# A Mamba block and a mixture-of-experts layer on one core: three of sixteen scan states weighted by C in channel layout and added to y by transfers instead of being transposed

## The chip, the core and the metric

One core of a Trainium2 chip runs the whole program. The metric is the device time of one execution in microseconds; lower is better. The kernel before took 2412.94 us (median of three runs, 2410.59 to 2414.03).

## What is computed

The reference takes a batch of 16 sequences of 512 tokens with 256 channels and applies two layers, each as `x + layernorm(layer(layernorm(x)))`. The first is a selective state-space (Mamba) layer, the second a gated low-rank mixture with a cumulative sum over time. The change lies in the first:

```
h = x * rsqrt(mean(x*x) + eps) * norm_scale @ w_in
xs, res = split(h);  res = silu(res);  xs = silu(causal_conv(xs) + conv_b)
delta, B, C = split(xs @ w_xproj);     delta = softplus(delta @ w_dt + b_dt)
deltaA = exp(delta * -exp(A_log));     deltaBx = delta * xs * B
ys = scan over time of (ys = deltaA * ys + deltaBx)      # 512 channels x 16 states
y  = sum over the 16 states of ys * C
out = (y + xs * D) * res @ w_out
```

All is float32.

## The kernel before

Layout. The 512 inner channels lie on the 128 partitions in four chunks c, time (512 steps) along the free dimension. The program keeps three stages in flight, each for another sequence: F (the front: norm, w_in, convolution, silu, delta, B, C), the scan over the 16 states, and B and L (the output projection, both layernorms, router, and the expert layer). Every engine runs one fixed, in-order program.

Order. `BEATS` is 128: a period of one sequence has 16 slots, one for each state n, and a slot has 8 beats. `TIMETABLE` (L96) gives each task of F, B and L on each engine a beat, modulo 128; `walk` (L391) runs for every beat first the engine's `scan_part` and then the tasks of that beat, for the sequence that is then in that stage. A beat is a place in the order and no time: engines meet only through semaphores.

The scan, for state n in slot n:

- ScalarE (L1260) computes `decay = exp(delta * rate)` for chunk c at beats 0, 2, 4, 6 into two PSUM tiles used in turn. It may be two chunks ahead of VectorE.
- GpSimd (L775) computes `bx = dx * B` for two chunks at a time at beats 0 and 4 into a ring of three (`BX_RING`), so it may be up to three half slots ahead. It needs the row of B for state n, spread over all partitions.
- SyncE (L611) loads that row from a scratch in DRAM into a ring of four (`BB_RING`), three slots ahead; `write_B` (L590) puts B there when F has computed it.
- VectorE (L1405) runs the scan of chunk c at beats 0, 2, 4, 6 into `h[n % 2]`, and at beats 1, 3, 5, 7 the products of the state before: `yT += stateT * C` (L1441), for four chunks of tokens.
- TensorE (L991) supplies these: it transposes `h` of the state before, four 128x128 blocks for each of four token chunks, into two PSUM tiles `stateT` used in turn. C is then one number per partition (`C_tok`).
- When all 16 states are summed, `y_task` (L889) transposes yT back, `u_task` (L1340) adds `xs * D`, and `o_task` on GpSimd multiplies by `res`.

In stage L, `cum_task` (L1230, ScalarE) writes `cum_sb`, `pr_task` (L1399, VectorE) multiplies into `prod`, and `pt_task` on TensorE transposes `prod`. For the first sequence `prod` also holds a piece of the raw weights. `rows` of the next sequence's B are loaded by the task `row`, w, w2, d1 and dx (L691 to L718) are the GpSimd steps that finish delta and `dx = delta * xs` for the next sequence, four chunks each, and `silu_task` (L1125) and `gelu_task` (L1209) are long blocks of ScalarE with a table load at both ends.

## Time and profile before

The profiled execution took 2413.96 us, with a span of 2412.2 us from the first to the last instruction.

| engine | busy us | share of the span | instructions |
|---|---|---|---|
| VectorE (DVE) | 2147.9 | 89% | 2775 |
| TensorE (PE) | 2143.7 | 89% | 9268 |
| GpSimd (POOL) | 1898.4 | 79% | 1369 |
| ScalarE (ACT) | 1839.0 | 76% | 3893 |
| DMA engines (16) | 14% of their time, all issued by SyncE | | |

How to read it: the shares include a filling and an emptying of the pipeline at both ends, in which VectorE is nearly idle, so the steady periods in between are fuller than the shares say. A duration in the profile runs until the instruction's last write; the next one on the same engine starts a little before that, so what an instruction costs its engine is the distance from start to start. A wait is put down to the instruction that came last.

### The profile page before, as it was taken

The numbers are of one execution on the slowest core, as the hardware profiler recorded it, in microseconds if no ns is written. First come the engines' busy times: TensorE is split into PE (matmuls) and PEld (weight loads), VectorE is DVE, ScalarE is ACT, GpSimd is POOL, SyncE is SP. The second block draws the span as 40 slices with busy tenths as digits, with TensorE's granted clock in tenths as the row PEclk, the third lists the DMA queues.
The fourth block names the chain that finished last, engine by engine and source line by source line (L and its number), as shares of the span: only waits on it lengthen the run. The fifth ranks groups of instructions, "written<-read, shape, count | busy, mean of one in ns | idle before, by whom it ended". The sixth has DMA issues, their size and how long they took to land.

```text
span 2412.2 us, 35956 instructions
## 1 busy us (share of the span) xinstructions
PE 2143.7 (89%) x9268; PEld 1300.3 (54%) x9268; DVE 2147.9 (89%) x2775; ACT 1839.0 (76%) x3893; POOL 1898.4 (79%) x1369
## 2 busy tenths in 40 slices
PE   5687899999998989899998999999898999998888
PEld 2455455564655556465655646565564656555454
DVE  2889999998999999999999989999999999999920
ACT  6675787869698787968778696978879797875644
POOL 1679797988889798888979888897988889796520
PEclk8796899898999989999999989999899999989899
DMA  6111101111111011111102011110211110011000
GB/s 135 36 45 39 45 32 32 58 31 54 37 57 33 27 61 30 54 36 58 33 27 62 30 52 37 58 36 23 64 32 54 36 58 31 26 51 35 27 9 9
DMA packets 83401, 101.70 MB, mean 42 GB/s; under 512 B 23480, under 2 KB 49872, under 8 KB 83168
## 3 DMA queue, kind: packets, MB, share of 16 engines
q1 hardware_dynamic: 83168, 99.06, 13.7%
q8 instruction: 89, 1.46, 0.2%
q14 instruction: 144, 1.18, 0.2%
HBM read 90.13 MB, written 8.91 MB: 41 GB/s over the span
## 4 chain that ended last, share of the span: by engine, by line
DVE 34%; issue 26%; PE 15%; ACT 13%; POOL 9%; DVEq 1%; ACTq 0%; POOLq 0%
DVE h L1425 15%; DVE yT L1441 11%; PE bank L827 7%; POOL bx L792 4%; PE stateT L1007 4%; ACT decay L1277 2%; DVE xs L1336 2%; PE bank L986 1%; DVE yT L1438 1%; POOL dx L718 1%; POOL delta L712 1%; ACT scratch L1207 1%; ACT res L1141 1%; ACT prodT L1064 1%; ACT o_rows L1045 1%
## 5 line engine op out<-in xcount | busy, mean ns | idle before, releaser
L792 POOL TENSOR_TENSOR bx<-dx,B_rows 128x1024 f32<-128x1024 f32 x512 | 1204.6, 2363 | 286.9 <-DVE h L1425 252.4
L1425 DVE TENSOR_TENSOR_SCAN h<-decay,bx 128x512 f32<-128x512 f32 x1024 | 1236.8, 1208 | 64.7 <-ACT decay L1277 51.9
L1277 ACT ACTIVATE decay<-delta,decay_rate 128x512 f32<-128x512 f32 x1024 | 702.4, 691 | 351.0 <-DVE h L1425 343.0
L1007 PE MATMUL stateT<-ident,h 128*128 128x128 f32 x4096 | 646.9, 291 | 176.2 <-DVE h L1425 119.3
L1007 PEld LDWEIGHTS stateT<-ident,h 128*128 128x128 f32 x4096 | 492.6, 148 | 523.4 <-issue 306.8
L1441 DVE SCALAR_TENSOR_TENSOR yT<-stateT,C_tok,yT 128x512 f32<-128x512 f32 x960 | 694.7, 724 | 47.7 <-PE stateT L1007 47.5
L827 PE MATMUL bank<-hT,w_in_sb 128*128 128x512 f32 x512 | 246.5, 611 | 23.5 <-DVE xs L1336 9.9
L827 PE MATMUL bank<-q_to_expert,xnT 128*128 128x512 f32 x512 | 261.5, 638 | 0.1
L827 PE MATMUL bank<-k_to_expert,cumT 128*128 128x512 f32 x512 | 258.4, 630 | 0.0
L986 PE MATMUL bank<-expert_to_out,prodT 128*128 128x256 f32 x1024 | 244.5, 382 | 6.4 <-issue 6.4
L1241 ACT ACTIVATE cum_sb<-bank,gate 128x64 f32<-128x64 f32 x1024 | 221.8, 326 | 22.9 <-PE bank L827 20.2
L986 PEld LDWEIGHTS bank<-expert_to_out,prodT 128*128 128x128 f32 x1024 | 185.8, 191 | 31.0 <-issue 10.9
L827 PEld LDWEIGHTS bank<-hT,w_in_sb 128*128 128x128 f32 x512 | 91.7, 194 | 106.5 <-issue 73.0
L827 PEld LDWEIGHTS bank<-q_to_expert,xnT 128*128 128x128 f32 x512 | 97.3, 207 | 80.1 <-issue 79.5
L827 PEld LDWEIGHTS bank<-k_to_expert,cumT 128*128 128x128 f32 x512 | 92.8, 202 | 78.7 <-issue 72.8
L827 PE MATMUL bank<-w_out_sb,res 128*128 128x256 f32 x512 | 121.9, 382 | 0.0
L688 POOL TENSOR_TENSOR xs<-xs,scratch 128x511 f32<-128x511 f32 (+2 forms) x93 | 106.8, 1148 | 18.4 <-ACT scratch L1110 12.3
L1403 DVE TENSOR_TENSOR prod<-bank,cum_sb 128x512 f32<-128x512 f32 x128 | 85.2, 665 | 37.0 <-PE bank L827 24.9
L827 PE MATMUL bank<-xnT,q_to_router 128*128 128x512 f32 x256 | 117.9, 594 | 0.0
L827 PEld LDWEIGHTS bank<-w_out_sb,res 128*128 128x128 f32 x512 | 94.5, 192 | 17.6 <-issue 7.2
L1251 ACT ACTIVATE prodT<-bank 128x512 f32<-128x512 f32 x128 | 75.9, 593 | 30.1 <-PE bank L986 25.3
L736 POOL TENSOR_TENSOR res<-xs,res 128x512 f32<-128x512 f32 x64 | 80.9, 1276 | 20.4 <-DVE xs L1343 20.4
(164 smaller groups left out, 2584.8 us busy)
## 6 DMA issues: line engine op xcount, KB each, us to landing
B_rows<-B_scratch SPq DMA_DIRECT2D x256, 256.0 KB, 3.2
x_front<-in_L_attn_x SPq DMA_DIRECT2D x16, 512.0 KB, 5.3
x_back<-in_L_attn_x SPq DMA_DIRECT2D x16, 512.0 KB, 3.5
out<-x_back SPq DMA_DIRECT2D x16, 512.0 KB, 5.8
w_in_sb<-in_L_attn_w_in SPq DMA_DIRECT2D x1, 1024.0 KB, 5.9
cum_sb<-in_L_ffn_V_fwd SPq DMA_DIRECT2D x2, 256.0 KB
prod<-in_L_ffn_W_inv_exp SPq DMA_DIRECT2D x2, 256.0 KB
xnT<-in_L_ffn_W_fwd SPq DMA_DIRECT2D x2, 256.0 KB
```

Of the source, the lines that this page charges most:

```text
L688: pool.tensor_tensor(xs[b.parity][:, c, back:], xs[b.parity][:, c, back:], scratch[:, tile, 0:T - back], ALU.add).then_inc(f_pool.step(f"c ...
L736: pool.tensor_tensor(res[r][:, c, :], xs[r][:, c, :], res[r][:, c, :], ALU.mult).then_inc(b_pool.step(f"o{c}"), 1)
L792: pool.tensor_tensor(bx[use % BX_RING][:, :, :], dx[q.parity][:, 2 * half:2 * half + 2, :], row, ALU.mult).then_inc(s_bx.step(f"{n},{half} ...
L827: last = pe.matmul(out_ap, lhsT, rhs, start=(i == 0), stop=(i == len(pairs) - 1))
L986: last = pe.matmul(use.bank[:, 0:D], prodT[:, 4 * br + i, :], expert_to_out[:, 4 * br + i, :], start=(br == 0 and i == 0), stop=False)
L1007: last = pe.transpose(stateT[j % 2][:, c * P:(c + 1) * P], h[n % 2][:, c, j * P:(j + 1) * P], ident[:, :])
L1241: last = act.activation(cum_sb[u % 2][:, k * RK:(k + 1) * RK], use.bank[:, k * RK:(k + 1) * RK], ACT.Copy, scale=gate[:, j, br * KE + k:br ...
L1251: act.activation(flat(prodT[:, 4 * br:4 * br + 4, :]), use.bank[:, :], ACT.Copy).then_inc(l_act.step(f"pt{u}"), 1)
L1277: act.activation(decay[c % 2][:, :], delta[q.parity][:, c, :], ACT.Exp, scale=decay_rate[:, c, n:n + 1]).then_inc(s_exp.step(f"{n},{c}"), 1)
L1403: dve.tensor_tensor(prod[u % 2][:, :], use.bank[:, :], cum_sb[u % 2][:, :], ALU.mult).then_inc(l_dve.step(f"pr{u}"), 1)
L1425: dve.tensor_tensor_scan(h[n % 2][:, c, :], decay[c % 2][:, :], bx[(2 * n + c // 2) % BX_RING][:, c % 2, :], 0.0, ALU.mult, ALU.add).then_ ...
L1441: ins = dve.scalar_tensor_tensor(out=yT[:, k, :], in0=stateT[k % 2][:, :], scalar=C_tok[batch.parity][:, k, n:n + 1], in1=yT[:, k, :], op0 ...
```

## The change

States 3, 7 and 11 (`MIXED`) are no longer transposed. For such a state n:

- SyncE loads the row of C for it, spread over the partitions, into `C_rows` (`row_of_C`, beat 4 of slot n-2); the scratch in DRAM now takes B and C.
- ScalarE copies `C_rows` into the PSUM tile `stateT[0]` at beat 7 of slot n (`spread_C`), after the product of state n-1 for token chunk 2 has read it.
- VectorE multiplies two chunks of `h` at a time by it in slot n+1: chunks 2 and 3 in place at beat 1, chunks 0 and 1 into `weighted` at beat 5 (`weigh_half`). The four products with `yT` fall away.
- GpSimd issues two transfers, 512 KB each, that add these halves to `xs` (`add_half`, `accum_op=ALU.add`): at beat 7 of slot n+1 and at beat 3 of slot n+2. Before the second it waits until the first has landed. VectorE's scan of state n+2, chunk 2, waits for the first to land, since it reads the same buffer.
- TensorE leaves out the 16 transposes of slot n+1.

So that `xs` can take these sums, ScalarE first scales it by D (`skip`, four tasks, after `dx`), and `u_task` is a plain addition. For the memory, `prod` goes (the product is written over `cum_sb`), and the ring of B rows has three places instead of four, so that the rows of B for states 0 and 1 of the next sequence are loaded early and row 0 must wait for `bx` of state 15. Many beats of the timetable are moved by some places.

```diff
-BB_RING = 4
+BB_RING = 3
+MIXED = (3, 7, 11)
+PLAIN = [n for n in range(NS) if n not in MIXED]
+C_AT, ADDED_AT = 7, (7, 3)
...
-    ("F", "silu", "act"): (67,),
+    ("F", "silu", "act"): (66,),
...
-    ("F", "w", "pool"): (97, 106, 120, 121),
-    ("F", "w2", "pool"): (99, 111, 123, 127),
-    ("F", "d1", "pool"): (102, 112, 127, 128),
-    ("F", "row", "sp"): (123, 127, 137),
+    ("F", "w", "pool"): (97, 103, 108, 123),
+    ("F", "w2", "pool"): (100, 105, 117, 124),
+    ("F", "d1", "pool"): (101, 107, 126, 126),
+    ("F", "row", "sp"): (113, 113),
...
+    ("F", "skip", "act"): (117, 122, 132, 132),
...
-    ("L", "pr", "dve"): (355, 368, 371, 384, 398, 430, 432, 438),
+    ("L", "pr", "dve"): (362, 371, 373, 387, 399, 425, 431, 441),
...
-    ("F", "dx", "pool"): (117, 118, 128, 129),
+    ("F", "dx", "pool"): (102, 123, 128, 131),
...
+            def add_half(q, n, half):
+
+                before = 2 * MIXED.index(n) + 1 - half
+                pool.wait_ge(s_mul.sem, s_mul.done(q, f"{n},{half}"))
+                pool.sem_inc(passed["pool"], 1)
+                if before == 0:
+                    pool.wait_ge(f_act.sem, f_act.done(q, "sk3"))
+                    pool.sem_inc(passed["pool"], 1)
+                if before or q.shift(-1).exists:
+                    pool.wait_ge(y_added, q.count(32 * len(MIXED), 16 * before))
+                    pool.sem_inc(passed["pool"], 1)
+                half_rows = flat(xs[q.parity][:, 2 * half:2 * half + 2, :])
+                source = flat(h[n % 2][:, 2:4, :]) if half else flat(weighted[:, :, :])
+                pool.dma_start(half_rows, source, accum_op=ALU.add).then_inc(y_added, 16)
+
             def scan_part(q, n, beat):
+                if q.exists and beat == ADDED_AT[0] and n - 1 in MIXED:
+                    add_half(q, n - 1, 1)
+                if q.exists and beat == ADDED_AT[1] and n - 2 in MIXED:
+                    add_half(q, n - 2, 0)
...
+            def spread_C(q, n):
+                act.wait_ge(C_in, q.count(16 * len(MIXED), 16 * (MIXED.index(n) + 1)))
+                act.sem_inc(passed["act"], 1)
+                act.wait_ge(s_acc.sem, s_acc.done(q, f"{n - 1},2"))
+                act.activation(stateT[0][:, :], C_rows[:, :], ACT.Copy).then_inc(s_C.step(f"{n}"), 1)
+
...
+            def weigh_half(q, n, half):
+
+                dve.wait_ge(s_C.sem, s_C.done(q, f"{n}"))
+                state = h[n % 2][:, 2 * half:2 * half + 2, :]
+                dve.wait_ge(s_scan.sem, s_scan.done(q, f"{n},{2 * half + 1}"))
+                if half == 0 and (MIXED.index(n) or q.shift(-1).exists):
+                    dve.wait_ge(y_added, q.count(32 * len(MIXED), 32 * MIXED.index(n)))
+                spread = stateT[0][:, :].rearrange("p (o t) -> p o t", o=1).broadcast_to([P, 2, T])
+                dve.tensor_tensor(state if half else weighted[:, :, :], state, spread, ALU.mult).then_inc(s_mul.step(f"{n},{half}"), 1)
...
                     if c == 0:
                         free = q if n >= 2 else q.shift(-1)
-                        if free.exists:
+                        if free.exists and n - 2 not in MIXED:
                             dve.wait_ge(s_tr.sem, s_tr.done(free, f"{(n - 2) % NS},{TB - 1}"))
+                    if c == 0 and n - 2 in MIXED:
+                        dve.wait_ge(s_mul.sem, s_mul.done(q, f"{n - 2},0"))
+                    if c == 2 and n - 2 in MIXED:
+                        dve.wait_ge(y_added, q.count(32 * len(MIXED), 32 * MIXED.index(n - 2) + 16))
...
+                if n in MIXED:
+                    if k % 2 == 0:
+                        weigh_half(batch, n, 1 - k // 2)
+                    return
```

## Rows read from the trace of the kernel before

**Rows 1.** Instructions on tile x_back: min/median/max ns, first and last start
```profile
L609 SPq MOVE out<-x_back x12: 29/29/29, 430.6 to 1969.6; - x12
```
**Rows 2.** Window: us, busy PE, PEld, DVE, ACT, POOL (count), clock, DMA share, GB/s
```profile
1115.00:1252.00 137.00, 127.20 (x562) 77.81 (x563) 130.63 (x170) 109.89 (x236) 119.99 (x86) 0.95 0.13 42
```
**Rows 3.** Waits between 430 and 2074 us: us in total, times, longest
```profile
DVE h L1425 <- ACT decay L1277: 39.2, 35, 1.7
DVE yT L1441 <- PE stateT L1007: 27.3, 29, 1.5
POOL bx L792 <- DVE h L1425: 158.5, 119, 5.0
```
**Rows 4.** VectorE's timeline in slots 12 and 13: start us, duration us, instruction
```profile
1145.93 0.68 DVE L1403 TENSOR_TENSOR prod<-bank,cum_sb 128x512 f32<-128x512 f32 x1
1146.53 1.21 DVE L1425 TENSOR_TENSOR_SCAN h<-decay,bx 128x512 f32<-128x512 f32 x1
1147.66 0.72 DVE L1441 SCALAR_TENSOR_TENSOR yT<-stateT,C_tok,yT 128x512 f32<-128x512 f32 x1
1148.31 1.21 DVE L1425 TENSOR_TENSOR_SCAN h<-decay,bx 128x512 f32<-128x512 f32 x1
```
**Rows 5.** Groups of instructions, VectorE: count | busy us, mean ns | idle before, releaser
```profile
L1441 DVE SCALAR_TENSOR_TENSOR yT<-stateT,C_tok,yT 128x512 f32<-128x512 f32 x960 | 694.7, 724 | 47.7 <-PE stateT L1007 47.5
L1357 DVE SCALAR_TENSOR_TENSOR rows<-x_back,r_keep,bank 128x256 f32<-128x256 f32 x64 | 29.5, 463 | 9.3 <-PE bank L827 9.3
```
**Rows 6.** VectorE's timeline, three waits of one period: in brackets the idle time before
```profile
1112.54 1.22 DVE L1425 TENSOR_TENSOR_SCAN h<-decay,bx 128x512 f32<-128x512 f32 x1 [1.45 <-ACT decay L1277]
1141.72 0.75 DVE L1441 SCALAR_TENSOR_TENSOR yT<-stateT,C_tok,yT 128x512 f32<-128x512 f32 x1 [1.23 <-PE stateT L1007]
1155.96 0.75 DVE L1441 SCALAR_TENSOR_TENSOR yT<-stateT,C_tok,yT 128x512 f32<-128x512 f32 x1 [1.13 <-PE stateT L1007]
```
**Rows 7.** TensorE's timeline: four transposes of a state
```profile
1180.07 0.60 PE L1007 MATMUL stateT<-ident,h 128*128 128x128 f32 x4
```
**Rows 8.** Groups of instructions, ScalarE, same columns
```profile
L1183 ACT ACTIVATE scratch<-scratch,one 128x512 f32<-128x512 f32 x64 | 46.3, 723 | 4.0
L1198 ACT ACTIVATE xnT<-bank 128x512 f32<-128x512 f32 x32 | 19.0, 594 | 0.1
```
**Rows 9.** Groups of instructions, GpSimd, same columns
```profile
L792 POOL TENSOR_TENSOR bx<-dx,B_rows 128x1024 f32<-128x1024 f32 x512 | 1204.6, 2363 | 286.9 <-DVE h L1425 252.4
L697 POOL TENSOR_TENSOR scratch<-scratch 128x512 f32<-128x512 f32 x60 | 76.0, 1272 | 0.5
```
**Rows 10.** GpSimd's timeline, its only waits for VectorE between 1273 and 1312 us
```profile
1273.25 2.38 POOL L792 TENSOR_TENSOR bx<-dx,B_rows 128x1024 f32<-128x1024 f32 x1 [0.41 <-DVE h L1425]
1309.56 2.36 POOL L792 TENSOR_TENSOR bx<-dx,B_rows 128x1024 f32<-128x1024 f32 x1 [0.94 <-DVE h L1425]
```
**Rows 11.** The page's DMA issues: count, KB each, us from issue to landing
```profile
B_rows<-B_scratch SPq DMA_DIRECT2D x256, 256.0 KB, 3.2
x_front<-in_L_attn_x SPq DMA_DIRECT2D x16, 512.0 KB, 5.3
x_back<-in_L_attn_x SPq DMA_DIRECT2D x16, 512.0 KB, 3.5
out<-x_back SPq DMA_DIRECT2D x16, 512.0 KB, 5.8
```
**Rows 12.** Instructions on tile x_back, columns as in group 1: the longest issue
```profile
L530 SPq DMA_DIRECT2D x_back<-in_L_ffn_U_inv x2: 1123/1134/1145, 28.1 to 29.3; - x2
```
**Rows 13.** SyncE's timeline: start us, duration us of a short issue
```profile
1129.57 0.39 SPq L589 DMA_DIRECT2D x_front<-in_L_attn_x  x1
```
**Rows 14.** Windows of 4 us in slots 11 and 13, columns as in group 2
```profile
1132.00:1136.00 4.00, 3.97 (x12) 2.68 (x12) 3.66 (x7) 3.97 (x8) 3.73 (x3) 0.50 0.91 302
1148.00:1152.00 4.00, 2.35 (x11) 2.06 (x12) 4.00 (x6) 3.83 (x7) 3.44 (x3) 0.52 0.22 70
1152.00:1156.00 4.00, 4.00 (x14) 2.16 (x13) 2.87 (x4) 3.87 (x8) 4.00 (x3) 0.63 0.00 0
```

More of the change, by code:

```diff
@@ L132 @@
-    ("B", "r", "dve"): (285, 289, 290, 291),
-    ("B", "st", "dve"): (293,),
+    ("F", "hT", "pe"): (21, 22),
+    ("F", "hT", "act"): (28, 29),
+    ("F", "x", "sp"): (90,),
+    ("F", "xs", "pe"): (29, 33, 36, 38),
+    ("F", "xs", "act"): (33, 35, 39, 42),
+    ("F", "cvA", "dve"): (32, None, 36, None),
+    ("F", "cvB", "dve"): (33, None, 37, None),
+    ("F", "cvC", "dve"): (34, None, 39, None),
+    ("F", "tap", "act"): (None, 37, None, 42),
+    ("F", "cv", "pool"): (None, 39, None, 62),
@@ new lines @@
+    ("F", "res", "pe"): (37, 41, 44, 55),
+    ("F", "res", "act"): (40, 50, 51, 59),
+    ("F", "silu", "act"): (66,),
+    ("F", "proj", "pe"): (77,),
+    ("F", "proj", "act"): (81,),
+    ("F", "B", "sp"): (85,),
+    ("F", "Ct", "pe"): (116,),
+    ("F", "Ct", "act"): (116,),
+    ("F", "dt", "pe"): (83, 85, 88, 104),
+    ("F", "dt", "act"): (87, 93, 104, 109),
+    ("F", "ex", "act"): (89, 97, 106, 110),
+    ("F", "ln", "act"): (91, 100, 106, 111),
+    ("F", "w", "pool"): (97, 103, 108, 123),
@@ L147 @@
+    ("B", "xnT", "act"): (318, 318),
+    ("B", "cum", "dve"): (319, 320),
+    ("B", "rt", "pe"): (320, 325, 325, 325),
+    ("B", "rt", "act"): (324, 325, 331, 331),
     ("B", "gelu", "act"): (334,),
@@ L289, in program @@
         cum_sb = [sb(f"cum_sb{i}", P, KR) for i in range(2)]
-        prod = [sb(f"prod{i}", P, KR) for i in range(2)]
+        weighted = sb("weighted", P, 2, T)
+        C_rows = sb("C_rows", P, T)
         prodT = sb("prodT", P, 8, P)
@@ L326, in program @@
         s_scan = Steps(sem("s_scan"), [f"{n},{c}" for n in range(NS) for c in range(CT)])
-        s_tr = Steps(sem("s_tr"), [f"{n},{c}" for n in range(NS) for c in range(TB)])
-        s_acc = Steps(sem("s_acc"), [f"{n},{c}" for n in range(NS) for c in range(TB)])
+        s_tr = Steps(sem("s_tr"), [f"{n},{c}" for n in PLAIN for c in range(TB)])
+        s_acc = Steps(sem("s_acc"), [f"{n},{c}" for n in PLAIN for c in range(TB)])
+        s_C = Steps(sem("s_C"), [f"{n}" for n in MIXED])
+        s_mul = Steps(sem("s_mul"), [f"{n},{half}" for n in MIXED for half in (1, 0)])
+        C_in, y_added = sem("C_in"), sem("y_added")
         b_pe = Steps(sem("b_pe"), steps_of("pe", "B", {"y": ["y{}"], "wo": ["wo{}"], "xnT": ["xnT{}"], "rt": ["rt{}"],
@@ L442, in walk @@
                 period(Batch(q))
-        stage_V = [cum_sb, prod]
+        stage_V = [cum_sb, [dx[1][:, t, :] for t in range(DT)]]
         stage_W = [[xnT[:, 0, :], xnT[:, 1, :]], [prodT[:, 4 * t:4 * t + 4, :].rearrange("p a b -> p (a b)") for t in range(DT)]]
@@ L609, in store, with row_of_C @@
                 sp.dma_start(batch.dram(out_rows), x_back[batch.parity][:, :, :]).then_inc(stored[batch.parity], 16)
+            def row_of_C(q, i):
+                free, last = (q, i - 1) if i else (q.shift(-1), len(MIXED) - 1)
+                if i == 0:
+                    sp.wait_ge(B_out, q.count(16, 16))
+                    sp.sem_inc(passed["sp"], 1)
+                if free.exists:
+                    sp.wait_ge(s_C.sem, s_C.done(free, f"{MIXED[last]}"))
+                    sp.sem_inc(passed["sp"], 1)
+                n = NS + MIXED[i]
+                sp.dma_start(C_rows[:, :], B_dram[q.parity, n:n + 1, :].partition_broadcast(P).rearrange("p o t -> p (o t)")).then_inc(C_in, 16)
             def scan_part(q, slot, beat):
+                if beat == 4 and q.exists and slot + 2 in MIXED:
+                    row_of_C(q, MIXED.index(slot + 2))
                 if beat == 0 and q.exists:
@@ L998, in scan_part @@
                     return
+                if n in MIXED:
+                    return
                 if j == 0:
                     pe.wait_ge(s_scan.sem, s_scan.done(batch, f"{n},{CT - 1}"))
-                back = n * TB + j - 2
+                at = PLAIN.index(n)
+                back = at * TB + j - 2
                 free = batch if back >= 0 else batch.shift(-1)
+                if j == 0 and n - 1 in MIXED:
+                    pe.wait_ge(s_mul.sem, s_mul.done(batch, f"{n - 1},0"))
+                    pe.sem_inc(passed["pe"], 1)
                 if free.exists:
-                    pe.wait_ge(s_acc.sem, s_acc.done(free, f"{back % (NS * TB) // TB},{back % TB}"))
+                    back %= len(PLAIN) * TB
+                    pe.wait_ge(s_acc.sem, s_acc.done(free, f"{PLAIN[back // TB]},{back % TB}"))
                 for c in range(CT):
@@ L1262, in scan_part @@
                     rates()
+                if q.exists and beat == C_AT and n in MIXED:
+                    spread_C(q, n)
                 if not q.exists or beat % 2:
```

123 lines of the change are left out of this document (54 added, 69 removed), and 6 rows, old and new, of the table TIMETABLE.

## Prediction

> **What bounds the kernel now.** I read the engines' shares first, then the period, then the waits. The stores of twelve inner sequences start 430.6 to 1969.6 us, so one sequence costs (1969.6 - 430.6) / 11 = 139.9 us [rows 1]. The scans of all 16 sequences run at about that rate, and a saving per period counts about 16 times; the filling and the emptying at the ends have little to do with the change. In a steady window VectorE is busy 130.6 of 137 us, TensorE 127.2, GpSimd 120.0, ScalarE 109.9 [rows 2]. Scaled to the period VectorE has 6.5 us of idle time, GpSimd 17, ScalarE 28. So VectorE is the bound, and its idle time says who holds it. From 430 to 2074 us (11.75 periods) it waited 39.2 us for ScalarE's decay, which is 3.3 a period, and 27.3 for TensorE's transposes, 2.3 a period [rows 3]. Of the first kind is the wait of 1.45 us at the silu block, of the second are those in slots 12 and 13 (1.23 and 1.13) [rows 6]. GpSimd waits 158.5 / 11.75 = 13.5 us a period for VectorE to free the ring [rows 3]: it is ahead, but the trace shows no such wait from 1273 to 1309.5, where the steps for the next sequence lie (slots 11 to 15) [rows 10]. There it has nearly nothing to spare.
>
> **VectorE's work.** From start to start a scan takes 1147.66 - 1146.53 = 1.13 us, a product with yT 0.65, and an addition or multiplication of 512 columns with one PSUM operand 0.60 [rows 4]. A multiplication over 1024 columns isn't in the trace. 256 columns more cost 724 - 463 = 261 ns in the mean durations [rows 5], so 512 more cost 0.52 and the new instruction 1.12, at least; the most is two of the old ones, 1.20. I take 1.13. Removed are 3 x 4 = 12 products, 7.80 us; added 3 x 2 = 6 weighings, 6.78; the four additions of u get cheaper by 0.05 each, 0.20. That is **-1.2 us a period** (bounds -0.8 to -1.3). The product of stage L costs the same; its buffer's wait moves to ScalarE.
>
> **TensorE.** 48 transposes of a period go, in 12 groups of four that take some 0.60 us each [rows 7], up to 7 us. VectorE's wait of 1.23 at slot 12 is for the transposes of state 11, which are left out; that of 1.13 in slot 13 comes after TensorE has fallen behind, and the missing slot-12 transposes give it 2.4 us. Of 2.3 us a period I expect all but 0.2 to go: **-2.1** (bounds -2.3 and 0, if TensorE's other tasks, moved by the timetable, take its place). What is late next is ScalarE.
>
> **ScalarE.** Three copies of C at 0.59 and four scalings of xs at 0.72 [rows 8] are 4.7 us of 28 idle. The copy in beat 7 of slot n can only start when VectorE is through beat 5; behind it on ScalarE is the decay for slot n+1, chunk 0, which VectorE needs after one scan and one product (1.78 us), against the copy's 0.59 and one decay of much the same size: a margin of some half a microsecond, which another ScalarE task in between uses up. Scaling chunk 1 (beat 122) waits for GpSimd's dx at beat 123, which is safe only while GpSimd is ahead. The silu block holds decay chunk 2 of slot 8 as before, since scan, weighing and cumulative scans take about the place of scan, product and cumulative scans. I take **+0.5** (bounds 0 and +2, the latter three lost margins and a late scaling).
>
> **SyncE.** Three C rows of 256 KB more, and row 0 of B must now wait for bx of state 15 and takes 3.2 us to land [rows 11]. GpSimd has three steps of 1.27 us [rows 9] between these two bx, 3.8 us, which hide it; without that cover it would cost up to 3.5 us a period. Nothing that is needed sooner stands behind the waiting load. Zero.
>
> **GpSimd and the transfers.** Six transfers a period that add are issued by GpSimd; the trace has none of that kind. Issue: between 0.39 and 1.13 us, the short and the long issue of SyncE [rows 12, 13]; I take 0.8, so 4.8 us of 17 idle. Landing, D: plain transfers of 512 KB take 3.5, 5.3 and 5.8 us [rows 11]; an adding one also reads its target, so the bounds are 3.5 and twice the longest, 11.6. I take 5.3, the one into SBUF that is slower, because SBUF on both sides saves a trip to DRAM and the second read costs some of that. Behind these waits on GpSimd's queue stand bx and the steps of the next sequence, and VectorE waits for bx. The Trainium skill, DMA: Bandwidth & Descriptors, section Anatomy of one DMA, gives 2.0 us plus the bytes at 436 GB/s for a transfer issued by GpSimd, an estimate of 3.2 us here; no transfer of this trace is issued so, and the sum by it would be -26 us or better in place of the -16 below.
>
> Let T be the end of VectorE's first weighing, in slot n+1. VectorE then has four scans (12,1), (12,2), (12,3), (13,0), a weighing, a product, scan (13,1) and a product before scan (13,2), which needs the second bx of state 13: 5 x 1.13 + 1.13 + 2 x 0.65 = 8.1 us, plus one task of stage L (0.60), so T + 8.7. GpSimd after T: issue 0.8, w 1.27, bx 2.36, w2 1.27, so T + 5.7; the landing is at T + 0.8 + D = 6.1; issue, d1 and bx, 0.8 + 1.27 + 2.36, end at T + 10.5. A **stall of 1.8 us** after state 11. After state 7 GpSimd has no steps of the next sequence: 6.1 + 0.8 + 2.4 = T + 9.3 against 8.1 + the silu wait of about 1.5 = 9.6, none. After state 3 three convolution sums of GpSimd and six taps of VectorE are both in the way: about T + 10 against 12, none. So **+1.8**; the other two bounds: D = 3.5 gives 1.4 (GpSimd's steps, not D, are then the limit), D = 11.6 gives 8.1 + 5.9 + 3.6 = 17.6.
>
> **Sum.** -1.2 - 2.1 + 0.5 + 1.8 = -1.0 us a period, times 16 = -16 us; the stall at slot 13 also gives ScalarE and TensorE time to catch up for the boundary, which I put at 0.2 a period, so -19. The profiled execution took 2413.96 us with a span of 2412.2, within 0.05% of the median 2412.94, so the sum can be put on the median: **2394 us** (-0.8%).
>
> **The rivals.** (a) *Landing is slow (slower).* The place is GpSimd's wait for the first half before it issues the second, with bx behind it. The stall after state 11 is D - 3.5, after state 7 D - 5.7, after state 3 D - 8. The other terms give -3.0 a period, so the sum turns at D = 6.1, where the first two make 3.0. At D = 8 they are 4.5 + 2.3 = 6.8, that is +3.8 a period, 2474 us; at 11.6 it is 2413 + 16 x 14.6 = 2647. For it: 6.1 is only 0.3 above a plain store. Against: SBUF is at both ends, and the DMA engines are 14% busy.
> (b) *TensorE's clock.* The granted clock is 0.50 from 1132 to 1136 and 0.52 from 1148 to 1152, that is 1.2 in place of 2.4 GHz; in the second case TensorE was busy only 2.35 of 4 us, and in the next window, at 0.63 with 4.00 busy, VectorE was left with 2.87 of 4 [rows 14] and waited 1.13 [rows 6]. The change takes 16 transposes out of slots 4, 8 and 12 and leaves holes there. With one more such stretch in each the 2.1 us stay and 3 x 1.2 come on top: -1.0 + 2.1 + 3.6 = +4.7 a period, 2488 us; with one more stretch, 2.3 a period, 2450. Against: stages F and L fill slot 4 and 12. The Trainium skill, TensorE: Matmul & The Clock Gate, Part 1, says that the throttled clock is the default and activity releases it; by that rule a relief of TensorE can be given back, and the row of 1148 agrees, that of 1132 (3.97 busy) doesn't by itself.
> (c) *Both hidden.* GpSimd does the steps while it would have waited for T, and the stall after state 11 is gone: -3.0 a period, 2365 us.
> (d) *Nothing moves.* ScalarE's bound (+2) and the stall eat the gain: -1.2 - 2.1 + 2 + 1.8 = +0.5, with the margins half kept, 0: 2413 us.
>
> **How the numbers follow.** Forecast 0.36, (c) 0.19, (a) 0.24, (b) 0.08, (d) 0.13. A difference of 0.2% (5 us) is about what a measurement of this kernel can tell from none. Faster is the forecast and (c), 0.55; within 0.2% is (d), 0.13; slower is (a) and (b), 0.32. The range goes from 2358, (c) with the best VectorE bound, to 2475, (a) at D = 8, which leaves out some 0.04 below and 0.13 above; the likeliest case's own range is 2375 to 2405.
>
> **What would show it.** VectorE's weighings at 1.1 to 1.2 us, six a sequence, its products at 52; the waits for TensorE nearly gone; a new wait of VectorE's scan for bx of 1.5 to 2 us in slot 13 and none in slots 5 and 9; transfers that land in 5 to 6 us; the clock no lower than before in slots 4, 8 and 12; period 138.7 us. I am wrong if D is above 6, if an issue holds GpSimd for much over a microsecond (each 0.5 us more adds a microsecond to the stall), or if ScalarE's waits double.

## The result and the profile after

The changed kernel took 2433.82 us (median of three runs, 2431.96 to 2435.19) against 2412.94: a ratio of 1.0082 with a 95% interval from 1.0067 to 1.0097, 21 us slower. The forecast was 19 us faster. The page of the kernel after, busy time of each engine with its share of the span:

```profile
PE 2070.9 (85%) x8500; PEld 1220.7 (50%) x8500; DVE 2134.0 (88%) x2679; ACT 1891.3 (78%) x4005; POOL 1982.2 (81%) x1465
```

The stores, which give the period as [rows 1] did:

```profile
L617 SPq MOVE out<-x_back x12: 29/29/29, 441.5 to 1992.7; - x12
```

The period is (1992.7 - 441.5) / 11 = 141.0 us, against 139.9. The last of the twelve stores is 23.1 us late: 10.9 of that is there at the first store, in the filling of the pipeline, and 12.2 comes in eleven periods of +1.1. So the sum of a period times 16, which I used, isn't the form of this loss: half of it is made in the first 430 us.

The stretch from 430 to 2074 us as one window, first the kernel before and then the one after (columns as in rows 2):

```profile
430.00:2074.00 1644.00, 1519.24 (x6726) 924.27 (x6726) 1566.55 (x2026) 1333.14 (x2851) 1414.08 (x1012) 0.96 0.14 43
```
```profile
430.00:2074.00 1644.00, 1455.11 (x6117) 857.02 (x6116) 1541.63 (x1931) 1365.84 (x2918) 1463.90 (x1074) 0.95 0.29 71
```

VectorE is busy 1566.55 / 11.75 = 133.3 us of 139.9 before and 1541.63 / 11.66 = 132.2 of 141.0 after (1644 us are 11.66 of the longer periods). It has 1.1 us less to do and 2.2 us more of idle time. Whom it waits for, in the same stretch (us in total, times, longest), is to be held against [rows 3]:

```profile
DVE h L1502 <- POOL bx L833: 39.7, 38, 2.0
DVE h L1502 <- ACT decay L1339: 37.3, 30, 2.0
DVE h L1502 <- DMA xs<-weighted: 14.8, 12, 1.3
DVE yT L1522 <- PE stateT L1055: 7.4, 10, 2.4
```

The waits for TensorE fell from 2.3 to 0.6 us a period. New is GpSimd: 39.7, and the 14.8 put down to a transfer is GpSimd's too, as the views of slots 12 and 13 below show. But of the 39.7, 12.2 us are six waits of 2.03 behind ScalarE's gelu block, where the same wait, as long, is put down to ScalarE in the other periods. VectorE's timeline at that place in two periods (start us, duration us, instruction, in brackets the idle time before it):

```profile
719.52 1.22 DVE L1502 TENSOR_TENSOR_SCAN h<-decay,bx 128x512 f32<-128x512 f32 x1 [2.03 <-POOL bx L833]
...
1141.41 1.22 DVE L1502 TENSOR_TENSOR_SCAN h<-decay,bx 128x512 f32<-128x512 f32 x1 [2.03 <-ACT decay L1339]
```

Both scans start 0.88 us after ScalarE started their decay (718.64 and 1140.53), so both waits are ScalarE's. Counted so, VectorE waits 39.7 + 14.8 - 12.2 = 42.3 us for GpSimd, 3.6 a period against 0.2 before, and 37.3 + 12.2 = 49.5 for ScalarE, 4.2 a period against 3.3. GpSimd's timeline in slots 12 and 13:

```profile
1157.59 1.27 POOL L740 TENSOR_TENSOR dx<-delta,xs 128x512 f32<-128x512 f32 x1
1159.24 0.93 POOL L810 DMA_DIRECT2D xs<-h  x1 [0.38 <-issue]
1159.93 1.55 POOL L719 TENSOR_TENSOR scratch<-scratch 128x512 f32<-128x512 f32 x1
1161.16 2.62 POOL L833 TENSOR_TENSOR bx<-dx,B_rows 128x1024 f32<-128x1024 f32 x1
1163.47 1.53 POOL L727 TENSOR_TENSOR scratch<-scratch,dx 128x512 f32<-128x512 f32 x1
1164.74 1.10 POOL L810 DMA_DIRECT2D xs<-weighted  x1
1165.35 1.79 POOL L734 TENSOR_TENSOR delta<-delta,scratch 128x512 f32<-128x512 f32 x1
1166.59 2.86 POOL L833 TENSOR_TENSOR bx<-dx,B_rows 128x1024 f32<-128x1024 f32 x1
1168.90 1.76 POOL L719 TENSOR_TENSOR scratch<-scratch 128x512 f32<-128x512 f32 x1
```

VectorE's timeline of the same microseconds:

```profile
1157.37 1.19 DVE L1476 TENSOR_TENSOR h<-h,stateT 128x1024 f32<-128x1024 f32 x1
...
1160.73 1.19 DVE L1476 TENSOR_TENSOR weighted<-h,stateT 128x1024 f32<-128x1024 f32 x1
1161.84 1.21 DVE L1502 TENSOR_TENSOR_SCAN h<-decay,bx 128x512 f32<-128x512 f32 x1
1163.90 1.22 DVE L1502 TENSOR_TENSOR_SCAN h<-decay,bx 128x512 f32<-128x512 f32 x1 [0.85 <-POOL bx L833]
...
1169.57 1.22 DVE L1502 TENSOR_TENSOR_SCAN h<-decay,bx 128x512 f32<-128x512 f32 x1 [1.29 <-DMA xs<-weighted]
```

The bx of slot 13 started at 1166.59 and ran 2.86 us, to 1169.45; the scan started at 1169.57. The transfer named beside it isn't what released it: by the code this scan waits only for the first of the two, which had landed near 1163.84, and with transfers of 8 KB, further down, the wait stays. And GpSimd had no wait in this stretch but 0.38, 0.7 us behind the first weighing (1157.37 + 1.19 = 1158.56): from there on it was late by its own work. VectorE's waits for it lie in three places (us in all periods, a period): slot 12 (10.2, 0.9), slot 13 (14.8, 1.3), and the turn to the next sequence (17.1, 1.5; the kernel before waits 6.2 us in all there, put down to others). After states 3 and 7 there is none to speak of. The second issue (1164.74) did not wait for the landing of the first (1159.24 + 4.6 = 1163.84).

What else answers to the prediction's rows: the two weighings, the two issues on GpSimd (count, busy us, mean ns, idle before) and the landings (count, KB, us):

```profile
L1476 DVE TENSOR_TENSOR h<-h,stateT 128x1024 f32<-128x1024 f32 x48 | 57.5, 1197 | 0.0
L1476 DVE TENSOR_TENSOR weighted<-h,stateT 128x1024 f32<-128x1024 f32 x48 | 57.5, 1197 | 0.0
...
L810 POOL DMA_DIRECT2D xs<-weighted x48 | 45.0, 937 | 37.6 <-DMA xs<-h 33.2 <-DVE weighted L1476 4.5
L810 POOL DMA_DIRECT2D xs<-h x48 | 44.8, 933 | 140.2 <-ACT scratch L1158 75.7 <-DVE h L1476 58.4 <-issue 6.1
```
```profile
xs<-h POOLq DMA_DIRECT2D x48, 512.0 KB, 4.6
xs<-weighted POOLq DMA_DIRECT2D x48, 512.0 KB, 4.8
```

### The profile page after: what moved, and what is told of

The parts are those of the page before. It is cut to its first block, busy times and chain, and to the rows that moved or that the text cites. A ratio compares the mean times of both kernels' runs of the same rounds, so it can differ in the third digit from the quotient of the medians.

```text
span 2433.4 us, 35919 instructions
## 1 busy us (share of the span) xinstructions
PE 2070.9 (85%) x8500; PEld 1220.7 (50%) x8500; DVE 2134.0 (88%) x2679; ACT 1891.3 (78%) x4005; POOL 1982.2 (81%) x1465
## 4 chain that ended last, share of the span: by engine, by line
DVE 29%; issue 26%; POOL 14%; PE 14%; ACT 11%; DVEq 2%; DMA 1%; POOLq 0%; ACTq 0%; SPq 0%
DVE h L1502 11%; PE bank L868 8%; DVE yT L1522 7%; POOL bx L833 6%; ACT decay L1339 3%; PE stateT L1055 3%; DVE xs L1398 2%; POOL scratch L719 2%; POOL scratch L727 2%; POOL dx L740 2%; POOL delta L734 2%; DVE yT L1519 1%; DVE xs L1407 1%; ACT res L1189 1%; DVE weighted L1476 1%
## 5 line engine op out<-in xcount | busy, mean ns | idle before, releaser
L833 POOL TENSOR_TENSOR bx<-dx,B_rows 128x1024 f32<-128x1024 f32 x512 | 1249.2, 2478 | 62.9 <-DVE dx L1369 31.9
L1055 PE MATMUL stateT<-ident,h 128*128 128x128 f32 x3328 | 545.6, 295 | 151.2 <-DVE h L1502 109.4
L1055 PEld LDWEIGHTS stateT<-ident,h 128*128 128x128 f32 x3328 | 406.6, 150 | 472.3 <-issue 311.6
L1522 DVE SCALAR_TENSOR_TENSOR yT<-stateT,C_tok,yT 128x512 f32<-128x512 f32 x768 | 557.2, 726 | 27.0 <-PE stateT L1055 24.6
L868 PE MATMUL bank<-k_to_expert,cumT 128*128 128x512 f32 x512 | 270.5, 655 | 8.6 <-DVE xs L1407 8.3
L1301 ACT ACTIVATE cum_sb<-bank,gate 128x64 f32<-128x64 f32 x1024 | 222.1, 328 | 31.4 <-PE bank L1013 21.6
L868 PE MATMUL bank<-q_to_expert,xnT 128*128 128x512 f32 x512 | 241.6, 595 | 0.0
L810 POOL DMA_DIRECT2D xs<-h x48 | 44.8, 933 | 140.2 <-ACT scratch L1158 75.7
L868 PEld LDWEIGHTS bank<-q_to_expert,xnT 128*128 128x128 f32 x512 | 90.8, 192 | 76.8 <-issue 73.2
L710 POOL TENSOR_TENSOR xs<-xs,scratch 128x511 f32<-128x511 f32 (+2 forms) x93 | 111.2, 1196 | 18.7 <-ACT scratch L1158 13.0
L1466 DVE TENSOR_TENSOR cum_sb<-bank,cum_sb 128x512 f32<-128x512 f32 x128 | 86.1, 673 | 37.0 <-PE bank L868 26.5
```

Source lines behind the costliest of these rows:

```text
L710: pool.tensor_tensor(xs[b.parity][:, c, back:], xs[b.parity][:, c, back:], scratch[:, tile, 0:T - back], ALU.add).then_inc(f_pool.step(f"c ...
L833: pool.tensor_tensor(bx[use % BX_RING][:, :, :], dx[q.parity][:, 2 * half:2 * half + 2, :], row, ALU.mult).then_inc(s_bx.step(f"{n},{half} ...
L868: last = pe.matmul(out_ap, lhsT, rhs, start=(i == 0), stop=(i == len(pairs) - 1))
L1055: last = pe.transpose(stateT[j % 2][:, c * P:(c + 1) * P], h[n % 2][:, c, j * P:(j + 1) * P], ident[:, :])
L1301: last = act.activation(cum_sb[u % 2][:, k * RK:(k + 1) * RK], use.bank[:, k * RK:(k + 1) * RK], ACT.Copy, scale=gate[:, j, br * KE + k:br ...
L1466: dve.tensor_tensor(cum_sb[u % 2][:, :], use.bank[:, :], cum_sb[u % 2][:, :], ALU.mult).then_inc(l_dve.step(f"pr{u}"), 1)
```

## The experiments

All ratios are to the kernel before, run beside it on the same chip (5 to 11 runs of each changed kernel; four chips in all), with the 95% interval. Differences under 0.2% between two of these ratios are not told apart by them.

### Is it the transfers?

My first theory was that the transfers and GpSimd make the loss. The transfers go and GpSimd's waits stay; the row of C goes to another buffer; the second transfer comes later; or the transfers shrink to 16 columns. The last tells the landing apart from the issue.

```diff
# no_transfer
-                pool.dma_start(half_rows, source, accum_op=ALU.add).then_inc(y_added, 16)
+                pool.sem_inc(y_added, 16)
# tiny_transfers
+                pool.dma_start(half_rows[:, 0:16], source[:, 0:16], accum_op=ALU.add).then_inc(y_added, 16)
# add_later
-C_AT, ADDED_AT = 7, (7, 3)
+C_AT, ADDED_AT = 7, (7, 5)
# row0_apart: row 0 of B is loaded into C_rows, which is free once spread_C of state 11 has read it
+                sp.dma_start(C_rows[:, :], B_dram[batch.parity, 0:1, :].partition_broadcast(P).rearrange("p o t -> p (o t)")).then_inc(B0_in, 16)
```

> The changed kernel, but GpSimd counts the semaphore up in place of issuing the six adding transfers (the three states are missing from y); its wait for the weighing stays. Theory that GpSimd is the bound from slot 12 to the next slot 0: its 5.6 us of issues a period and the landing waits go, VectorE's waits for bx shrink from 4.7 to 1 to 2 us a period: 2370 to 2385. Rival that the moved timetable, the scaling on ScalarE and the ring cost the time: 2420 to 2434.

Measured 1.0044 [1.0027, 1.0061], 2424.0 us, period 140.6.

> The changed kernel with six adding transfers of 16 columns instead of 1024 (y is incomplete). If their issue on GpSimd is what costs: as the change, 2430 to 2434. If landing and traffic cost: as without transfers, 2424. By the rows the waits for a landing are 21.0 us in twelve periods, after state 7 only, where VectorE waits for ScalarE anyway: 2428 to 2432.

Measured 1.0073 [1.0059, 1.0087], 2431.7 us.

> The changed kernel with the second transfer at beat 5 in place of 3, behind the second bx of the slot. The wait of 1.29 us in slot 13 should shrink by the issue (0.9 us). Theory that GpSimd is work-bound up to the boundary: the same work comes a little later, the boundary waits stay, 5 to 10 us off: 2424 to 2429. If the place of that transfer is the cause: all of 1.29 x 16 = 20 us off, 2413.

Measured 1.0088 [1.0075, 1.0101], 2436.4 us.

> The changed kernel, but row 0 of B of the next sequence goes into C_rows (free between states 11 and 3) and no longer waits for bx of state 15. Ring theory: GpSimd's wait of 1.32 us before the first bx of a sequence goes and with it most of VectorE's 1.68, 1.3 us in 15 periods, 20 us: 2414. Rival, GpSimd is simply late there (its steps, not the row): it would only begin 1.3 us sooner with the same work behind it, and the later stalls grow: 0 to 5 us off, 2429 to 2434.

Measured 1.0081 [1.0067, 1.0095], 2433.2 us.

So the six transfers cost 0.4% in all, some 10 us, the larger part of it by their issue; what their size adds (1.0082 against 1.0073) isn't clear of zero. Even without them the kernel is 11 us slower than before. For the place of the second transfer, where my theory had 5 to 10 us, and for the row of B, where it had 20, no gain came. The groups of GpSimd for bx, first without transfers and then with tiny ones, show what an issue does (count, busy us, mean ns, idle before):

```profile
L833 POOL TENSOR_TENSOR bx<-dx,B_rows 128x1024 f32<-128x1024 f32 x512 | 1200.3, 2361 | 179.1 <-POOLq L810 98.7 <-DVE h L1502 47.4 <-DVE dx L1369 32.0
```
```profile
L833 POOL TENSOR_TENSOR bx<-dx,B_rows 128x1024 f32<-128x1024 f32 x512 | 1251.2, 2481 | 67.3 <-DVE dx L1369 32.0 <-DVE h L1502 28.6 <-issue 6.5
```

The mean record of bx grows from 2361 to 2481 ns with transfers of only 8 KB, as much as in the changed kernel; it is the issue and not the traffic. VectorE's waits without transfers, 430 to 2074 us:

```profile
DVE h L1502 <- ACT decay L1339: 50.1, 35, 2.0
DVE yT L1522 <- PE stateT L1055: 21.6, 25, 2.4
DVE h L1502 <- POOL bx L833: 10.9, 22, 1.3
DVE h L1502 <- PE stateT L1055: 8.5, 11, 1.7
```

Of the 42.3 us that VectorE had waited for GpSimd 31 are gone, and 23 of them come back as waits for TensorE (7.4 to 21.6 + 8.5 = 30.1); those for ScalarE are the same (49.5 and 50.1). With GpSimd as the late engine the waits for TensorE were covered: before it was 27.3 + 2.6 = 29.9 us, so without the transfers 48 fewer transposes a period bring no relief at all in this order.

### What do the surroundings cost, and what the three states?

```diff
# unmixed: the changed kernel, all states transposed
-MIXED = (3, 7, 11)
+MIXED = ()
# two_states
+MIXED = (3, 7)
# before_ring3: the kernel before
-BB_RING = 4
+BB_RING = 3
-    ("F", "row", "sp"): (123, 127, 137),
+    ("F", "row", "sp"): (123, 127),
```

> The kernel before with a ring of three B rows and nothing else. If the smaller ring costs by itself: 1.3 us a period or more, 2433 and above, and the transfers are innocent. If it only costs where GpSimd's lead is already gone: the row comes 2 us late, but VectorE needs it 5 us later, 2413 to 2418.

Measured 1.0000 [0.9992, 1.0009].

> The changed kernel with no state taken out (MIXED empty): all 16 states are transposed, nothing is weighted or transferred, but the moved timetable, the scaling of xs on ScalarE, the product over cum_sb and the ring of three rows stay. If these are free and the three states cost the time: 2413 or a little below (u gets 0.2 us a period cheaper). If they cost it: 2425 to 2440. The kernel without transfers stands at 1.0044 of before, so part of the loss, 10 us, lies either here or in the waits for the weighing and in TensorE's hole of slot 12.

Measured 1.0238 [1.0224, 1.0251], 2470.4 us, period 143.7.

> The changed kernel with states 3 and 7 only. Theory that the third state costs because GpSimd has no lead from slot 12 on (waits for bx of 0.85, 1.29, 1.68 and 0.56 us a period follow it): these 3 to 4 us go, the third of VectorE's gain (0.4) too, and TensorE's waits of slots 12 and 13 come back (1 to 2): 1 to 2 us a period, 2405 to 2418. Rival, each state costs alike: 2427.

Measured 1.0063 [1.0050, 1.0076], 2429.4 us.

This turned the question round. Given the changed kernel's surroundings, the three states bring 2470.4 - 2433.8 = 37 us: they are a gain. Two states bring 41, so the third brings nothing, or takes 4 us back; the two intervals overlap. The surroundings, which I had costed at nothing, lose 57 us. The ring of three isn't among them. Left are the merged product, the scaling by D on ScalarE, and the beats.

### Which of the surroundings?

Each was put into the kernel before alone:

```diff
# before_merged
-                dve.tensor_tensor(prod[u % 2][:, :], use.bank[:, :], cum_sb[u % 2][:, :], ALU.mult).then_inc(l_dve.step(f"pr{u}"), 1)
+                dve.tensor_tensor(cum_sb[u % 2][:, :], use.bank[:, :], cum_sb[u % 2][:, :], ALU.mult).then_inc(l_dve.step(f"pr{u}"), 1)
# before_skip (ScalarE scales, VectorE adds)
+    ("F", "skip", "act"): (120, 122, 132, 132),
...
-                dve.scalar_tensor_tensor(out=xs[r][:, c, :], in0=xs[r][:, c, :], scalar=skip_sb[:, c:c + 1],
-                                         in1=use.bank[:, :], op0=ALU.mult, op1=ALU.add).then_inc(b_dve.step(f"u{c}"), 1)
+                dve.tensor_tensor(xs[r][:, c, :], use.bank[:, :], xs[r][:, c, :], ALU.add).then_inc(b_dve.step(f"u{c}"), 1)
# before_new_beats: the changed kernel's beats for every task that both kernels have
-    ("L", "pr", "dve"): (355, 368, 371, 384, 398, 430, 432, 438),
+    ("L", "pr", "dve"): (362, 371, 373, 387, 399, 425, 431, 441),
...
```

> The kernel before with one part of the change: the product of stage L goes over cum_sb, and ScalarE's next cum waits for the transposes of the product instead of the product. Merging theory (the lost buffer is a main cost of the surroundings): 2430 to 2460. If it is free, as the prediction took it: 2410 to 2416.

Measured 1.0174 [1.0160, 1.0189], 2457.8 us.

> The kernel before with another part: xs scaled by D on ScalarE (four activations a period, 2.9 us), u a plain addition, the first sums of F six beats later. If ScalarE's 28 idle us hide it: -0.2 us a period, 2408 to 2414. If it sits on decay's path at the boundary: 2425 to 2440.

Measured 0.9983 [0.9974, 0.9991], 2408.0 us. It is the fastest kernel of this study.

> The kernel before with the beats of the change and nothing else (all its buffers, the ring of four, no scaling). If the order alone costs the 57 us by which the changed kernel without its three states is slower than before: 2450 to 2470. If the buffers cost it: 2413 to 2430.

Measured 1.0255 [1.0242, 1.0268], 2472.6 us.

The beats alone make the whole loss of the surroundings: 60 us against 57, not told apart. The merged product, "costs the same" in my text, costs 1.7%, over 40 us, in the old order: ScalarE must now wait until TensorE has transposed the product before it may write `cum_sb` again, 37.4 us between 430 and 2074. In the new order no cost of it can be seen, as this pair shows:

```diff
# no_transfer_prod: no_transfer, with prod back as a buffer of its own; the halves are weighed in place
+                dve.tensor_tensor(prod[u % 2][:, :], use.bank[:, :], cum_sb[u % 2][:, :], ALU.mult).then_inc(l_dve.step(f"pr{u}"), 1)
```

> The kernel without transfers once more (2424, 1.0044), but with prod as a buffer of its own and the old waits of stage L, in the room of weighted (both halves are weighted in place; y lacks three states). Merging theory: ScalarE's and TensorE's waits shrink, 2395 to 2412, below before. If the new order has absorbed the lost buffer: 2420 to 2425.

Measured 1.0057 [1.0038, 1.0077], 2427.7 us, against 1.0044 with the product merged.

### Would the change be faster in the old order?

```diff
# old_beats: the changed kernel, with the beats of the kernel before
-    ("F", "cv", "pool"): (None, 39, None, 62),
+    ("F", "cv", "pool"): (None, 45, None, 64),
...
# states_old_beats: the same, with prod apart and without transfers
# all_parts_old_beats: with prod apart and with transfers; one half is weighed into x_front
+        prod = [sb(f"prod{i}", P, KR) for i in range(2)]
+        weighted = x_front[:, :, :].rearrange("p a b -> p (a b)").rearrange("p (c t) -> p c t", c=2)
# two_states_old_beats: the last one with two states; the next x is loaded at beat 92 and not 112
+MIXED = (3, 7)
```

> The changed kernel, three states taken out as in the change, with the beats of the kernel before for all old tasks (save the first sums of stage F, which must stand behind the scaling). If the moved beats cost the time: below 2425, down to 2395 where the prediction's sum is right otherwise. If they were needed for the change: above 2434, since w2 and d1 of slots 15 and 16 and the wait for the three steps meet the transfers; ScalarE's cum tasks now wait for the transposes of the product: 2440 to 2470.

Measured 1.0664 [1.0650, 1.0677], 2575.0 us.

> What the prediction's sum for VectorE, TensorE and ScalarE speaks of, alone: the beats of the kernel before, prod as a buffer of its own, xs scaled on ScalarE, three states weighted in place and no transfer (y lacks them; GpSimd still waits for the weighings). The sum says -1.2 - 2.1 + 0.5 - 0.2 = -3.0 a period and no stall of GpSimd: 2365. The rival, that GpSimd's wait for the weighing alone takes its lead away where w, w2, d1 and dx lie in the old order: 2400 to 2440.

Measured 1.0385 [1.0371, 1.0400], 2505.9 us, period 146.5.

> The whole change with the old beats and without the merged product: weighted lies in x_front (free from slot 3 on, the next x is loaded at beat 112 behind the last transfer), so prod stays. If the merged product was what made the old beats slow (2575): this comes to the states' own value plus the issues, 2390 to 2420. If the old order doesn't go with the waits for the weighings: above 2434.

Measured 1.0658 [1.0643, 1.0672], 2571.3 us.

> The same with states 3 and 7 only, so that nothing is added to GpSimd in slots 12 and 13 where it is full: if its fullness there decides, below the three-state one and below before, 2385 to 2405; if the wait for the weighing costs in every slot, 2415 to 2430.

Measured 1.0338 [1.0324, 1.0352], 2496.6 us.

All four came out slower than any figure that was expected of them; only the signs "above 2434", that the old order doesn't go with the change, came true. `states_old_beats` is the test of my sum, since it is the sum: the kernel before with VectorE's saving, TensorE's relief and ScalarE's tasks, and no transfer (the ring of three rows is in it too). I had -3.0 us a period for it without the stall. It is +6.6. Its waits from 430 to 2074 us:

```profile
POOL bx L833 <- POOLq L810: 227.5, 67, 5.7
...
PE stateT L1055 <- DVE h L1503: 93.8, 52, 5.0
...
DVE yT L1523 <- PE stateT L1055: 54.1, 58, 2.4
DVE h L1503 <- ACT decay L1340: 44.7, 42, 2.4
...
DVE h L1503 <- POOL bx L833: 31.7, 23, 2.0
```

Its GpSimd timeline around slots 10 to 13, the waits for the weighings alone:

```profile
1119.22 2.36 POOL L833 TENSOR_TENSOR bx<-dx,B_rows 128x1024 f32<-128x1024 f32 x1 [3.50 <-POOLq L810]
1125.58 2.36 POOL L833 TENSOR_TENSOR bx<-dx,B_rows 128x1024 f32<-128x1024 f32 x1 [4.00 <-POOLq L810]
...
1159.04 2.36 POOL L833 TENSOR_TENSOR bx<-dx,B_rows 128x1024 f32<-128x1024 f32 x1 [3.41 <-POOLq L810]
1167.02 6.98 POOL L833 TENSOR_TENSOR bx<-dx,B_rows 128x1024 f32<-128x1024 f32 x3 [5.62 <-POOLq L810]
```

And TensorE's, the same period:

```profile
1168.11 0.65 PE L1055 MATMUL stateT<-ident,h 128*128 128x128 f32 x4 [3.56 <-DVE h L1503]
```

In the kernel before GpSimd stood ahead of VectorE and waited 158.5 us for a free place of the ring, 13.5 a period [rows 3]; such a wait costs nothing, since it is the lead itself. The adding step puts GpSimd six times a period behind a weighing of VectorE's, and as it runs ahead it stands there 227.5 / 11.2 = 20 us a period, with bx and the steps for dx behind it: the lead is gone. What VectorE itself waits longer for is bx, 2.8 us a period against 0.2, TensorE's transposes, (54.1 + 11.4) / 11.2 = 5.8 against 2.5, and ScalarE's decay, 4.0 against 3.3. For bx the path is shown; the larger part, TensorE's, which waits for scans 93.8 us here and 62.7 before, the runs show but don't explain. With the transfers (`all_parts_old_beats`) it waits only 7.3 us for bx but 107.9 for ScalarE's decay, and there GpSimd's lateness comes by way of ScalarE, which stands 31.9 us for GpSimd's `delta` and 32.9 for its `nm_b` and did for neither before. ScalarE's timeline, and then VectorE's, which waits for the decay behind these:

```profile
1087.80 0.72 ACT L1248 ACTIVATE scratch<-scratch,one 128x512 f32<-128x512 f32 x1 [2.84 <-POOL delta L738]
...
1163.48 2.08 ACT L1097 ACTIVATE rows<-rows,nm_b,rs_b 128x256 f32<-128x256 f32 x4 [3.00 <-POOL nm_b L679]
```
```profile
1090.52 1.22 DVE L1509 TENSOR_TENSOR_SCAN h<-decay,bx 128x512 f32<-128x512 f32 x1 [3.19 <-ACT decay L1344]
...
1166.32 1.22 DVE L1509 TENSOR_TENSOR_SCAN h<-decay,bx 128x512 f32<-128x512 f32 x1 [2.08 <-ACT decay L1344]
```

In `no_transfer`, the same steps of GpSimd in the new order, the waits for the weighings are 61.6 + 58.0 = 119.6 us (at L710 and L833), half as much. And the 61.6 stand before the convolution sums of slot 4, where the new order without any weighing waits 82.7 us for ScalarE (`unmixed`): the new order has a wait there anyway. So the moved beats have a use: they make the kernel with weighted states and no transfers 2428 us (`no_transfer_prod`) where it is 2506 in the old order, though they cost the kernel without such states 60 us. Putting prod apart and leaving it merged differ by nothing in the old order with states (1.0658 and 1.0664; the first also loads x later, for which no engine is seen to wait), though the merging cost 1.7% there without them. With two states the old order costs 84 us and with three 159, so GpSimd's full slots 12 and 13 alone are not the cause.

### Which of the moved beats?

```diff
# new_front_beats: the kernel before with the new beats of stage F
-    ("F", "cv", "pool"): (None, 45, None, 64),
+    ("F", "cv", "pool"): (None, 39, None, 62),
...
# new_late_front: of these, from beat 81 on
-    ("F", "w", "pool"): (97, 106, 120, 121),
+    ("F", "w", "pool"): (97, 103, 108, 123),
...
# new_back_beats: the kernel before with the new beats of stages B and L
-    ("B", "gT", "pe"): (361,),
+    ("B", "gT", "pe"): (358,),
...
```

> The kernel before with the new beats of stage F only (w, w2, d1, dx, convolution, hT, silu), those of B and L as before. If the steps of GpSimd and ScalarE for the next sequence make the new order slow (2473 with all of it): 2440 to 2470. If it is the order of L's matmuls and cum tasks: 2410 to 2425.

Measured 1.0274 [1.0260, 1.0288], 2479.2 us.

> The kernel before with the new beats of stage F from beat 81 on alone (dt, ex, ln, w, w2, d1, dx, Ct, B, proj: the steps that finish delta and dx for the next sequence); F's earlier beats, B and L as before. The new beats of all of F gave 1.0274, all new beats 1.0255. Theory (the steps that make dx are where GpSimd and ScalarE wait in a cycle with VectorE): 1.02 to 1.03, with GpSimd's waits for ScalarE's scratch near 70 us in the 1644 us of periods. Rival (the earlier beats of F: the TensorE, ScalarE and VectorE tasks of the convolution cost it): 1.00 to 1.01 here. Both in parts: 1.01 to 1.02.

Measured 1.0197 [1.0183, 1.0211], 2460.7 us.

> The kernel before with the new beats of stages B and L alone, F's as before. If the loss of the new order (1.0255) lies wholly in F's beats, 1.000 within 0.002. If it is a mismatch of one half with the other, whichever is moved, 1.01 to 1.03, and VectorE waits for TensorE's transposes as in the run with F's new beats (63 us). If these beats are of use by themselves, 0.99 to 0.998.

Measured 1.0318 [1.0304, 1.0332], 2488.9 us.

F's new beats cost 2.7%, B's and L's 3.2%, both together 2.6%. Costs that added up would have given near 5.9%, so they don't belong to single beats: whichever half is moved against the other loses. In all three runs the waits of VectorE for TensorE double (56.3 with all of F); that of the late half of F, then that of B and L, against 27.3 in [rows 3]:

```profile
DVE yT L1441 <- PE stateT L1007: 54.6, 55, 2.2
```
```profile
DVE yT L1441 <- PE stateT L1007: 59.5, 39, 3.9
```

With both halves moved (`before_new_beats`), as slow a kernel, they don't:

```profile
DVE h L1425 <- ACT decay L1277: 51.7, 51, 1.6
DVE yT L1441 <- PE stateT L1007: 26.6, 45, 3.7
```

There VectorE waits longer for ScalarE's decay (51.7 against 39.2), for bx (10.6 against 2.8) and for two others that it doesn't wait for in the old order (7.6 + 5.4). So the same loss sits in other waits, and a wait that doubles in the halves isn't the cause of the whole.

One place can be named. With the new beats of B and L `gT` takes the PSUM bank that a `cum` of stage L used last, and ScalarE must have emptied it. In the order before it stands at beat 105, its bank was last used by a `dt` of stage F, and it has no wait. At its new beat 102 TensorE stops for it once a sequence. The instruction's tile in `new_back_beats`, what TensorE sat idle for:

```profile
  ACT cum_sb L1241: 67.0, 16
```

And in the changed kernel, with the stretches around it as windows (columns as in rows 2):

```profile
1153.70 1.88 PE L868 MATMUL bank<-q_to_expert,xnT 128*128 128x512 f32 x4
1161.15 1.02 PE L990 MATMUL bank<-ident,gate 128*16 128x128 f32 x4 [5.57 <-ACT cum_sb L1301]
```
```profile
1152.62:1161.30 8.68, 3.11 (x14) 1.55 (x13) 8.68 (x11) 7.70 (x19) 8.30 (x9) 0.89 0.44 118
1161.43:1170.10 8.67, 7.51 (x21) 3.95 (x20) 6.48 (x8) 8.56 (x21) 8.67 (x7) 0.53 0.55 103
```

TensorE did 3.11 us of work in 8.68, and in the next 8.67 us its granted clock was 0.53, near the lower level of 1.2 GHz. But with all new beats and no states this wait is 7.0 us in the whole run (`before_new_beats`; 7.6 in `unmixed` and in `two_states`), and the kernels without states are the slower ones. So the long stop comes with the third state, or with half of the new order alone, and is no part of the 2.6%, which I can't put down to single tasks.

## Why the prediction was wrong, by its own steps

- **VectorE's work: right.** -1.2 was forecast, -1.1 came (133.3 to 132.2). The weighing's record is 1197 ns and its distance to the next start 1.11 to 1.13 (1161.84 - 1160.73), where I took 1.13.
- **TensorE's waits: near by the number, which was luck.** 2.3 to 0.6 a period against 0.2 forecast. Without the transfers they are 2.6 again: what hid them was GpSimd's lateness. My own bound of 0, "if TensorE's other tasks, moved by the timetable, take its place", is what this comes to, and I had given it no weight; that the timetable is the reason isn't shown, since in the old order (`states_old_beats`) they grow to 5.8.
- **ScalarE: somewhat too low.** +0.5 was forecast, +0.9 came (39.2 to 49.5 us), and +1.0 without transfers. The scaling by D, taken alone with VectorE's cheaper additions, gains 0.2% (`before_skip`). I had named the copy of C only as a lost margin, in the bounds: ScalarE idles 59.8 us in the whole run before its 48 copies, all but 0.1 of it on VectorE. What of the +0.9 is the copy's isn't shown.
- **SyncE and the ring of B: right,** zero, by `before_ring3` and `row0_apart`.
- **GpSimd: the term of the sum that was mis-sized.** +1.8 was forecast, 3.6 - 0.2 = +3.4 came. Landing was well placed (5.3 forecast, 4.6 and 4.8 measured), and rival (a), slow landing, falls: transfers of 8 KB change the time by 2 us. The issue has a record of 0.93 us but takes 0.6 to 0.7 from start to start, less than my 0.8. That states 3 and 7 cost nothing was right. After state 11 the chain came nearly as I wrote it: with T = 1158.56 the second bx of slot 13 ends at T + 10.9 (10.5 forecast) and VectorE is ready at T + 9.7 (8.7 forecast, and a wait of 0.85 in slot 12 that I had missed), which makes 2.1 us a period for both slots. The failed step is that I ended there and gave the stall back as time to catch up. GpSimd doesn't catch up in slots 13 to 15, where the steps of the next sequence lie, and holds VectorE again at the turn (1.68 us at 1191.15), 1.5 us a period where I had a gain of 0.2.
- **"The product of stage L costs the same; its buffer's wait moves to ScalarE": wrong in the order in which I summed.** A buffer that goes was costed at nothing, without naming who waits for it and what is late next. It is +1.7% in the old order and nothing in the new one.
- **The moved beats, costed at nothing: the largest error, and the step that failed first.** They cost 60 us without the states (`before_new_beats`) and save 78 with them (2505.9 to 2427.7), both times without transfers and with prod apart. I read them as slips of some places, and each was; but beats are the order of five in-order queues. And my sum took its waits from the trace of the old order: there the states cost 93 us without any transfer, +6.6 a period where I had -3.0.
- **The sum times 16: half right.** Eleven periods carry 12.2 of 23.1 us; 10.9 is made before the first store. `before_new_beats` has its first store at 440.2, so 9.6 of this comes with the beats. In the window from 130 to 200 us, VectorE is busy 61.09 us before and 54.84 after (55.24 without the transfers).
- **Rival (b), the clock: its stretch is there, its price isn't.** The clock is at 0.53 for 8.67 us in slot 13, behind the stop at `gT`; in slots 4 and 8 of that period, which the rival named too, it is at 1.00 (1085 to 1094 and 1120 to 1129 us). Over the periods it is 0.95 against 0.96, and VectorE's waits for TensorE fell all the same. No run tests the clock alone. The Trainium skill, TensorE: Matmul & The Clock Gate, Part 1, has activity release the clock; the two windows around the stop agree with it.
- **The estimate from the skill.** By the Trainium skill, DMA: Bandwidth & Descriptors, section Anatomy of one DMA, a landing would be near 3.2 us, an estimate. The adding transfers of this run take 4.6 and 4.8 and those of 8 KB 2.2; the measurement decides, and since `tiny_transfers` gains only 2 us, the time would hardly have differed.

In one sentence: the durations were right, and the order in which they meet was left out. The change's three states gain 37 us in an order that suits them, and that order, which is part of the change, costs 57 to 60.

What stays open: which tasks make the two halves of the order depend on each other (the stop at `gT` is one for the new half of B and L alone), why TensorE's waits grow with the states in the old order, and whether an order exists in which the three states beat the kernel before. None of the eleven kernels with weighted states did; the nearest are 1.0044 and 1.0057 without transfers, where y lacks the three states, and 1.0063 with two states.

## What to carry to other kernels

Where engines run fixed orders and one change moves many places in them, the sum of durations says little: measure the new order without the new work, and the new work in the old order, before arguing about either. A wait of an engine for its ring's consumer is its lead, and a step that makes it wait for that consumer at a late point spends the lead each time, even when the step itself is free. Every buffer that is dropped and every "costs the same" has to be priced by who waits for it next, in the order that will run.
